# A two-layer transformer on one core: one order table replaced by another, and a row of four small transfers shared between SyncE and ScalarE

## The reference, cut to what matters

```python
def _L0_cond_ref(x, cond, ...):
    ada = jax.nn.silu(cond) @ ada_w.T + ada_b
    g1, g2, s1, s2, sh1, sh2 = [a[:, None, :] for a in jnp.split(ada, 6, axis=-1)]
    h = _ln(x) * (1.0 + s1) + sh1
    ...
    scores = jnp.einsum('bqhd,bkhd->bhqk', q, k) * scale      # q, k after rope
    attn = jax.nn.softmax(scores, axis=-1)
    o = jnp.einsum('bhqk,bkhd->bqhd', attn, v).reshape(B, L, C)
    x = x + (o @ proj_w.T + proj_b) * g1
    h2 = _ln(x) * (1.0 + s2) + sh2
    ff = jax.nn.gelu(h2 @ fc1_w.T + fc1_b, approximate=True) @ fc2_w.T + fc2_b
    return x + ff * g2

def _L1_cond_ref(x, time_emb, ...):      # rmsnorm, the same attention, then
    x = x + _ffn(h, w_fc, b_fc, w_fo, b_fo)      # a * silu(gate), no gates g1, g2
```

## Time and profile before

| what | us |
|---|---|
| median of 3 runs (lowest, highest) | 814.12 (813.14, 817.34) |
| the profiled execution, its own time | 814.24 |
| its span, first to last instruction | 812.4 |
| TensorE busy | 741.3 |
| VectorE busy | 695.8 |
| ScalarE busy | 449.2 |
| GpSimd busy | 288.0 |

### The profile page before, as it was taken

The page is one execution under the profiler, slowest core; times in us unless marked ns, Lnnn a source line. Parts: engine busy times, 40 slices in busy tenths (PEclk is TensorE's granted clock), DMA queues, the critical chain, the costliest instruction groups (busy, mean ns, idle before and its releaser), DMA issues.

```text
span 812.4 us, 13189 instructions
## 1 busy us (share of the span) xinstructions
PE 741.3 (91%) x4576; PEld 452.9 (56%) x4576; DVE 695.8 (86%) x1177; ACT 449.2 (55%) x681; POOL 288.0 (35%) x267
## 2 busy tenths in 40 slices
PE   4989888999989989799988999899999999999697
PEld 4463234456545654366535655376746666567397
DVE  4578899999998998899999999989888999966555
ACT  1215564677647764477645766556545644564332
POOL 0411204345254245432453344412453223323154
PEclk9968898999999999899998999899999999999999
DMA  8280523521311232313113034413111122200001
GB/s 323 81 209 17 156 76 88 147 67 41 90 41 54 60 80 84 91 27 106 40 40 83 21 82 118 117 40 92 40 41 53 40 75 83 67 1 1 1 2 52
DMA packets 32882, 59.42 MB, mean 73 GB/s; under 512 B 7856, under 2 KB 12080, under 8 KB 32560
## 3 DMA queue, kind: packets, MB, share of 16 engines
q1 hardware_dynamic: 32816, 58.58, 25.1%
HBM read 39.42 MB, written 18.87 MB: 72 GB/s over the span
## 4 chain that ended last, share of the span: by engine, by line
PE 45%; DVE 33%; issue 10%; ACT 5%; DMA 3%; POOL 1%; SPq 1%; POOLq 0%; ACTq 0%; DVEq 0%
DVE top L1043 14%; PE ring L848 11%; PE ps_o L800 7%; PE ps_b L865 5%; PE ring L742 5%; PE ring L785 5%; PE ring L770 5%; DVE mlp L1131 4%; PE ring L755 3%; DMA mlp<-in_w_split 2%; ACT pr L1313 2%; DVE act_h L1145 2%; DVE xn L989 1%; DVE mlp L1152 1%; DVE xn L992 1%
## 5 line engine op out<-in xcount | busy, mean ns | idle before, releaser
L1043 DVE TENSOR_REDUCE top<-ring 128x2 fp32r<-128x1024 f32 x256 | 304.2, 1214 | 20.1 <-PE ring L785 19.1
L1313 ACT ACTIVATE pr<-ring 128x1024 f32<-128x1024 f32 x256 | 253.6, 1024 | 119.2 <-PE ring L770 105.9
L1447 POOL TENSOR_TENSOR act_l<-mlp,act_h 128x256 fp32r<-128x256 f32 x128 | 100.9, 788 | 254.3 <-DVE act_h L1145 254.3
L800 PE MATMUL ps_o<-pr,va 128*17 128x512 f32 x1024 | 134.8, 611 | 1.4 <-ACT pr L1313 1.2
L770 PE MATMUL ring<-qt,kt 49*128 49x512 f32 x512 | 112.9, 465 | 19.8 <-DVE top L1043 7.1
L785 PE MATMUL ring<-kt,qt 48*128 48x512 f32 x512 | 113.5, 469 | 11.3 <-DVE top L1043 5.7
L1327 ACT ACTIVATE mlp<-ring,col 128x256 f32<-128x256 f32 x128 | 60.8, 475 | 93.3 <-PE ring L848 70.7
L770 PEld LDWEIGHTS ring<-qt,kt 49*128 49x128 f32 x512 | 46.8, 186 | 103.8 <-issue 46.2
L785 PEld LDWEIGHTS ring<-kt,qt 48*128 48x128 f32 x512 | 47.9, 192 | 79.9 <-issue 26.3
L1131 DVE SCALAR_TENSOR_TENSOR mlp<-mlp 128x256 f32<-128x256 f32 x128 | 63.0, 492 | 26.7 <-ACT mlp L1334 24.9
L848 PE MATMUL ring<-hh,wl 128*128 128x256 f32 x384 | 82.8, 298 | 2.4 <-DVE top L1043 1.2
(11 more groups left out here) (83 smaller groups left out, 1018.3 us busy)
## 6 DMA issues: line engine op xcount, KB each, us to landing
scratch<-high SPq DMA_DIRECT2D x16, 512.0 KB, 3.9
scratch<-low SPq DMA_DIRECT2D x16, 512.0 KB, 4.3
qt<-scratch SPq DMA_DIRECT2D x64, 128.0 KB, 2.6
kt<-scratch SPq DMA_DIRECT2D x64, 128.0 KB, 2.7
mlp<-in_w_split SPq DMA_DIRECT2D x20, 256.0 KB, 3.2
qt<-scratch SPq DMA_DIRECT2D x64, 64.0 KB, 2.6
kt<-scratch SPq DMA_DIRECT2D x64, 64.0 KB, 2.7
xs<-in_x SPq DMA_DIRECT2D x4, 512.0 KB, 4.0
```

The lines of the kernel that those rows point to most:

```text
L800: last = nc.tensor.matmul(ps_o[32 * h:32 * h + HD + 1, :], va[:, u % 2, t, QUAD * g + h, :], pr[:, slot, :], start=(t == 0), stop=(t == T ...
L1043: nc.vector.tensor_reduce(top[:, n % 2, 0:4 * T].rearrange("p (e c) -> p e c", e=2)[:, :, c], pair[:, :, :], AX_X, ALU.max, negate=True).t ...
L1313: nc.scalar.activation(pr[:, at % NP:at % NP + 2, :], pair[:, :, :], ACT.Exp, scale=SCALE).then_inc(free, 1)
L1447: nc.gpsimd.tensor_tensor(act_l[:, at % 2, :], src, act_h[:, at % 2, :].bitcast(F32), ALU.subtract).then_inc(act_l_in, 1)
```

## The change

**Transfers.** The row of maxima is still written by four transfers. SyncE issues the first two, ScalarE the other two, in a new piece `("act", "top", n)` that waits for the same transposed maxima. The semaphore and the count that TensorE waits for stay.

```diff
-    pieces += [("dve", "top", n), ("sp", "top", n)]
+    pieces += [("dve", "top", n), ("sp", "top", n), ("act", "top", n)]
...
+        def top_parts(n, blocks):
+
+            for a in blocks:
+                yield (qt[SHIFT:SHIFT + STACK + 1:STACK, n % NSLOT, :, :].rearrange(
+                    "e h (t a q) -> e (h t) a q", t=T, a=P // BLOCK)[:, :, a, :].bitcast(F32),
+                       top_t[a * BLOCK:a * BLOCK + 4 * T, n % 2, :].bitcast(F32))
...
                     sp.wait_ge(top_turned, n + 1)
-                    for a in range(P // BLOCK):
-                        sp.dma_start(qt[SHIFT:SHIFT + STACK + 1:STACK, n % NSLOT, :, :].rearrange(
...
+                    for part in top_parts(n, range(2)):
+                        sp.dma_start(*part).then_inc(top_in[n % 2], 16)
...
+                def top_row(n):
+
+                    ac.wait_ge(top_turned, n + 1)
+                    for part in top_parts(n, range(2, P // BLOCK)):
+                        nc.scalar.dma_start(*part).then_inc(top_in[n % 2], 16)
...
-                                      "split_w": split_w, "take": take, "high": lift, "scores": scores,
+                                      "split_w": split_w, "take": take, "high": lift, "top": top_row, "scores": scores,
```

**Order.** All numbers of `ORDER` are new, and with them the order of pieces on every engine and the banks of the ring. No pass is added or taken away, and none changes its shape. A line of the table, before and after:

```diff
-        ("act", "split_w"): (6, 7, 8, 112, 123, 144, 220, 271, 272, 287, 324, 328, 1364, 1365, 1375, 1391, 1392, 1421,
+        ("act", "split_w"): (29, 90, 124, 137, 138, 154, 155, 171, 176, 220, 221, 306, 1401, 1403, 1416, 1417, 1441,
```

More of the change, by code:

```diff
@@ new lines @@
+        ("dve", "half_gate"): (22,),
+        ("dve", "silu"): (6,),
+        ("pe", "mod_0"): (2, 40),
+        ("dve", "norm_stats"): (1, 288, 72, 585, 249, 849, 516, 1146, 775, 1428, 1098, 1670, 1367, 1907, 1546, 2095,
+        2103),
+        ("dve", "norm_var"): (8, 293, 74, 609, 263, 853, 550, 1147, 811, 1444, 1110, 1671, 1389, 1909, 1605, 2097,
+        2111),
+        ("pool", "root"): (0, 289, 54, 608, 239, 951, 549, 1084, 897, 1404, 1063, 1656, 1337, 1924, 1614, 2022, 2023),
+        ("dve", "mod_0"): (11, 69),
@@ new lines @@
+        ("dve", "norm_rows"): (10, 313, 79, 616, 267, 865, 559, 1162, 832, 1459, 1120, 1694, 1400, 1925, 1659, 2108,
+        2115),
+        ("pe", "norm_turn"): (3, 349, 103, 628, 272, 891, 569, 1184, 839, 1478, 1134, 1714, 1419, 1928, 1673, 2099,
+        2100),
+        ("act", "modulated"): (12, 14, 339, 340, 95, 97, 623, 624, 277, 278, 887, 888, 560, 566, 1182, 1183, 841, 842,
[3 rows of a table added]
+        ("act", "take"): (18, 28, 38, 56, 101, 117, 169, 170, 286, 287, 337, 338, 574, 576, 617, 618, 846, 851, 862,
@@ new lines @@
+        863, 1139, 1148, 1155, 1166, 1426, 1430, 1452, 1453, 1676, 1677, 1679, 1693),
+        ("dve", "cosine"): (17, 52, 123, 182, 301, 347, 594, 625, 864, 889, 1152, 1193, 1432, 1507, 1683, 1729),
+        ("pool", "sine"): (20, 47, 99, 195, 292, 318, 584, 634, 953, 954, 1102, 1107, 1380, 1446, 1684, 1685),
+        ("dve", "rotate"): (24, 58, 130, 184, 319, 377, 595, 656, 866, 896, 1172, 1204, 1463, 1569, 1697, 1735),
+        ("act", "high"): (30, 61, 142, 208, 332, 381, 604, 660, 873, 901, 1174, 1223, 1473, 1627, 1708, 1831),
@@ new lines @@
+        ("pool", "low"): (35, 50, 127, 211, 304, 407, 588, 740, 958, 969, 1143, 1218, 1438, 1568, 1687, 1773),
[5 rows of a table added]
+        ("dve", "take_v"): (25, 37, 49, 59, 121, 144, 146, 210, 302, 303, 320, 321, 577, 590, 600, 601, 872, 877, 882,
+        885, 1173, 1176, 1177, 1180, 1457, 1458, 1467, 1469, 1689, 1690, 1706, 1707),
+        ("dve", "widen"): (34, 57, 65, 70),
+        ("pe", "gates"): (45, 51, 55, 64),
+        ("dve", "gates"): (62, 66, 77, 78),
+        ("pe", "net_1"): (19,),
+        ("dve", "net_1"): (33,),
@@ new lines @@
+        ("act", "net_gate"): (44,),
+        ("dve", "net_gate"): (41,),
+        ("pe", "net_2"): (43, 46, 53, 63, 67, 73, 82, 83),
+        ("dve", "net_2"): (108,),
+        ("sp", "load"): (23, 13, 27, 16, 39, 9, 32, 68, 89, 315, 284, 88),
+        ("sp", "load_w"): (26, 85, 98, 105, 109, 162, 163, 199, 237, 324, 325, 379, 1309, 1310, 1326, 1334, 1335,
+        1348, 1358, 1366),
+        ("act", "split_w"): (29, 90, 124, 137, 138, 154, 155, 171, 176, 220, 221, 306, 1401, 1403, 1416, 1417, 1441,
@@ new lines @@
+        1443, 1448, 1460),
+        ("dve", "split_w"): (114, 116, 145, 147, 158, 165, 166, 191, 264, 342, 343, 344, 1421, 1422, 1423, 1431, 1437,
+        1442, 1454, 1492),
+        (None, "scores"): (111, 118, 125, 126, 132, 133, 140, 148, 152, 159, 160, 174, 178, 180, 186, 187, 190, 194,
[13 rows of a table added]
+        (None, "peaks"): (80, 81, 84, 87, 92, 93, 94, 96, 104, 106, 110, 112, 113, 119, 122, 129, 136, 149, 150, 153,
[13 rows of a table added]
+        ("dve", "top"): (102, 131, 181, 217, 245, 298, 363, 452, 527, 573, 643, 727, 795, 856, 910, 1012, 1080, 1142,
[3 rows of a table added]
@@ new lines @@
+        ("dve", "back"): (215, 262, 484, 551, 747, 820, 1008, 1115, 1271, 1396, 1565, 1650, 1791, 1884, 2058, 2083),
+        ("pe", "project"): (268, 269, 270, 271, 563, 564, 565, 570, 829, 830, 834, 835, 1129, 1131, 1132, 1133, 1406,
+        1407, 1408, 1413, 1665, 1666, 1667, 1672, 1894, 1895, 1896, 1897, 2091, 2094, 2096, 2098),
+        ("dve", "residual"): (274, 276, 453, 561, 567, 568, 737, 822, 836, 837, 1014, 1122, 1125, 1135, 1300, 1394,
+        1409, 1418, 1588, 1661, 1662, 1664, 1821, 1890, 1892, 1893, 2012, 2086, 2087, 2102, 2164, 2197),
@@ new lines @@
+        ("pool", "residual"): (273, 275, 511, 556, 557, 581, 922, 923, 924, 948, 1058, 1079, 1081, 1082, 1304, 1342,
+        1346, 1356, 1630, 1653, 1654, 1655, 1919, 1920, 1921, 1922, 1980, 2143),
+        ("dve", "split_h"): (348, 354, 627, 629, 899, 900, 1186, 1187, 1489, 1490, 1722, 1723, 1930, 1934, 2114, 2119,
+        2128, 2129),
+        ("pool", "split_h"): (314, 316, 621, 622, 967, 968, 1160, 1161, 1450, 1451, 1725, 1726, 1935, 1936, 2028,
[8 rows of a table added]
+        ("act", "hidden"): (364, 365, 380, 384, 406, 408, 426, 428, 441, 459, 465, 485, 486, 506, 520, 521, 644, 646,
[6 rows of a table added]
@@ new lines @@
+        ("dve", "cube"): (362, 366, 383, 388, 402, 410, 420, 421, 445, 457, 476, 492, 493, 504, 524, 526, 650, 651,
+        659, 668, 687, 688, 703, 708, 724, 734, 741, 751, 770, 771, 792, 800, 909, 918, 926, 930, 941, 949, 980, 981,
+        1007, 1011, 1030, 1044, 1062, 1064, 1072, 1083, 1207, 1208, 1226, 1232, 1243, 1244, 1274, 1275, 1285, 1297,
+        1302, 1327, 1328, 1352, 1370, 1371),
+        ("act", "tanh"): (368, 374, 382, 394, 409, 411, 431, 433, 448, 470, 481, 487, 500, 512, 531, 533, 647, 653,
```

86 lines of the change are left out of this document (13 added, 73 removed), and 155 rows, old and new, of the table ORDER.

## The result

| | us |
|---|---|
| before, median of 4 runs (lowest, highest) | 813.63 (812.92, 817.34) |
| after, median of 4 runs (lowest, highest) | 778.66 (777.26, 780.14) |
| ratio, 95% interval | 0.956 (0.952 to 0.960) |
| span of the profiled execution after | 775.4 |

The change makes the kernel 35 us faster.

What follows compares the result with a forecast made beforehand. VectorE and TensorE were taken to share the bound from 100 to 520 us, TensorE alone after. Start -6, VectorE's passes -14, SyncE's shorter transfers -1, ScalarE's issues +2 gave -19 from 814.24: 795 us, range 780 to 816.

Steps and rivals of the forecast that it cites:

- the second term of the sum: VectorE's SBUF passes meet GpSimd's less often in the new order: -14 us at the end, bounds -3 and -32.
- 23 us of VectorE's time: VectorE's time saved by fewer meetings with GpSimd's passes, between 10 and 34 us.
- The transfers' +2: Two of four transfers issued on ScalarE, 64 issues taking 34 us, 5% of it costing: +2 us, between 0 and +34.
- The start: `hf` made before three weight copies on ScalarE, first reduction of maxima earlier: -6 us, between 0 and -8.3.
- The pattern: VectorE's SBUF passes wait for GpSimd's pass to end; the new order has fewer such places, saving 23 us of VectorE's time.
- The five lines: VectorE's `xn` of layer 0, `xn` of layer 1, casts, weight splits and `scaled`: together 34.0 us over their medians.
- The 34.0 us: VectorE's busy time less count times median, five lines, 60 to 520 us: the cost of waiting for GpSimd.
- How much of it reaches the end: 0.6: Share of VectorE's saved time that shortens the kernel: 0.6, the middle between a third (chain) and 94% (busy share).
- ScalarE holds the ring: Rival: ScalarE's issues wait for transposed maxima, exponentials behind keep PSUM banks, TensorE and VectorE starve: 818 to 834 us, chance 0.14.
- TensorE takes back what VectorE gives: Rival: TensorE is full from 100 to 520 us, so only the start counts: 809 us, between 805 and 810, chance 0.17.
- The waits change sides or places: Rival: VectorE's passes meet other GpSimd passes, or GpSimd is held instead: 810 to 818 us, chance 0.13.

Runs made afterwards that it cites:

- after_sp4: The changed kernel with all four transfers of a row of maxima issued by SyncE again, ScalarE's piece doing nothing: 757.55 us, ratio 0.932 to the kernel before.
- before_small_rest: The kernel before with GpSimd's sines, `low`, gate product, `xs` and `hl` cut to one eighth of their columns, `act_l` whole: 771.49 us, ratio 0.951.
- before_rows_first: The kernel before with the four `add` exchanged with the four `xn` behind each in VectorE's order, no more: 807.65 us, ratio 0.994.
- before_more: The kernel before with one of the eight reductions of maxima of each quad done twice: 845.75 us, ratio 1.041.

## Why the prediction was right or wrong

**The step that failed** is the second term of the sum, -14 for VectorE's passes, in both of its factors: 23 us of VectorE's time, and 0.6 of it at the end. The runs show 43 us in its place (695.8 to 652.5 in `after_sp4`), and 47 to 49 us at the end (the 55 of the order less 5.5 to 8 for the start). The transfers' +2 was wrong by 17 us the other way. That 795 lies no further than 16 us from 778.66 is therefore luck: the two errors, some 34 and 17 us, cancel in part.

**The start: right.** -6 was forecast; alone it measured -5.5, and `hf` came 8.0 us earlier (8.3 was the bound).

**The pattern: right, VectorE's share of it mis-sized.** VectorE's passes over SBUF wait for GpSimd's, and the order decides how often. "23 us of VectorE's time, between 10 and 34" was too little: VectorE lost 41.8 us of busy time, more than the upper bound. The five lines gave 35.5: the table leaves the casts 39.7 - 128 x 0.294 = 2.1 us over their median and `scaled` 2.1, and the others nothing, where I had left a third of the excess standing. Another 9 us came from `hidden`, `cube` and the cosine part, whose tails I had not looked at. The 34.0 us were an undercount from the start: they stand for five lines in one stretch, where the run with GpSimd's passes cut finds 61.2 us over all lines and the whole span. Count times median is also too much for passes whose records overlap: four undisturbed `xn` take 1.38 us, not 4 x 0.41 = 1.63. I had counted patterns of neighbours in the list, one by one; which meetings that count missed was not traced. The rule that I cited from the Trainium skill ("SBUF — State Buffer", "Who interferes with whom"), that one of the two engines waits for the whole pass of the other, agrees with the traces: `xn` fell from 2445 ns at most to 550 in `before_small_rest`, and the reductions, which read PSUM, had a median of 1.22 us and a longest of 1.23 in every kernel. I had used it as a reason for expecting that waits would only change sides; GpSimd's busy time is 288.0 us before and 288.6 after, so that they did not go over to it.

**"How much of it reaches the end: 0.6": wrong.** It was a middle between a share of the chain and a busy share, and neither measures it. The two runs with added reductions give 1.0, in the old order and in the new one, although TensorE is busy for 92% (before) to 98% (`after_sp4`) of 100 to 520 us; the runs that cut GpSimd's passes in the old order give 0.9. Two smaller gains, `before_rows_first` and the cut in the new order, give 0.5, so that 0.6 is not far off for a single step and wrong for the whole order. A busy TensorE is not a TensorE without slack: it pays for a late VectorE by standing still, and its granted clock is lower in windows with gaps: a mean of 0.83 of full speed from 320 to 340 us before the change, around the gap of the earlier trace rows, and 1.00 in the 20 us before and behind. From 100 to 520 us the granted clock is 0.98 in the earlier trace rows and 1.00 after; over the span it is 0.962 before, 0.960 in `before_more`, 0.979 in `before_small_rest` and 0.984 in `after_sp4`. TensorE's whole busy time fell by 22.8 us from before to `after_sp4` (741.3 to 718.5) for the same 4576 matmuls. How much of the gain is this and how much is standing still was not separated.

**Transfers, "+2, between 0 and +34": mis-sized by 17 to 19 us.** Inside its bounds, at the wrong end. I took 5%, ScalarE's part of the chain before, as the share of its issues that costs. The issues took what I had read from SyncE's row (0.52 us against 0.53), and some 57% of them reached the end (19 of 33 us). At the place shown, ScalarE's idle time does not lie behind the transposed maxima, where tanh, `hidden`, cast and `act_l` follow each other from engine to engine. The price of the rival "ScalarE holds the ring" was thus nearly the 62% at which it was to decide, and its mechanism is seen in part: TensorE waits longer for banks that exponentials hold, and the MLP's passes are late as well, which the rival did not name. It did not decide because the gains were 55 us, not 21. That the waiting for the transposed maxima would hold ScalarE was wrong: the wait alone costs nothing.

**The rival "TensorE takes back what VectorE gives"** does not hold for the order as a whole, by the added reductions and by `before_small_rest`; of the two smaller gains about half was lost on the way. "The waits change sides or places" holds in part for the single exchange, where 3.2 of 9.0 us came back as idle time, and not for the whole order.

**The sum as measured:** the start -5.5 to -8, VectorE's 43 us at 0.9 to 1.0, the transfers +19: -25 to -32 of the -35. Left are 3 to 10 us, which may lie in the rest of the order; the runs are uncertain by 2 to 3 us each, and I do not explain them.

## What to carry to other kernels

Where a busy engine's passes have long tails over a firm median, the tails can be waits, as here, though the profile counts them as busy; look for the other engine's pass that ends with them, and try an operation on another memory behind it instead. What a microsecond more on an engine costs is measured by adding a known, undisturbed amount to it, in one run; neither busy shares nor the chain's shares say it. What a microsecond less gains needs a run of its own, 0.5 to 0.9 here. An issue of a transfer takes its place in the list of the engine that makes it. ScalarE, with a third of its time free, had only some 0.35 to 0.5 us in each quad to spare in the middle of a chain that goes round several engines: keep issues on an engine that computes nothing, here the version with all four on SyncE, at 0.932 of the time before where the change as it was made has 0.956.

## What the runs showed of the hardware

A transfer's issue took 0.52 us on ScalarE (the median of 64; the shortest 0.50, the longest 1.63) and 0.53 us on SyncE. In the timeline after the change ScalarE does no work of its list while two issues last, 1.08 us, and the profile counts the time neither as busy nor as waiting for the issue. A pair of plain passes of 0.83 us cost on the same scale as issues do.

Behind a GpSimd pass VectorE does not slow down but stands: `xn`, 0.41 us, took up to 2.45 us, and with `low` and `sines` cut to an eighth at most 0.55 us. Of the four `xn` of the earlier trace rows, the first and the last took 0.41 and 0.40 us, and the two between them these:

```profile
328.47 2.44 DVE L989 TENSOR_SCALAR xn<-xs,mv,rstd 128x256 f32<-128x256 f32 x1
...
330.83 2.42 DVE L989 TENSOR_SCALAR xn<-xs,mv,rstd 128x256 f32<-128x256 f32 x1
```

They ended 0.15 and 0.14 us after `low` (330.76) and `sines` (333.11).
